# A small FFN on token halves: two column tiles and two row tiles of TensorE, sixteen half-length ReLUs and sums

## What is computed

```python
def ffn(x, Win, bin_, W1, b1, W2, b2, Wout, bout):      # M = 64, INNER = 16
    s = einsum('btd,dm->btm', x, Win) + bin_
    h = relu(s[..., None] * W1 + b1)                     # (tokens, 64, 16)
    g = einsum('btmh,mh->btm', h, W2) + b2
    return einsum('btm,md->btd', g, Wout) + bout

x = x + 0.5 * ffn(layernorm(x), ...)
x = x + attention_and_mlp(layernorm(x), ...)             # DFF = 2048, gelu
x = x + 0.5 * ffn(layernorm(x), ...)
```

## Time and profile before

| | |
|---|---|
| median of 3 runs | 3515.68 us (3514.63 to 3520.36) |
| the profiled execution | 3515.62 us |
| its span, first to last instruction | 3513.6 us |
| mean granted TensorE clock | 0.974 of full |
| TensorE (PE) busy | 3297.1 us, 94% |
| VectorE (DVE) busy | 1833.6 us, 52% |
| ScalarE (ACT) busy | 1322.4 us, 38% |
| GpSimd (POOL) busy | 1154.8 us, 33% |

### The profile page before, as it was taken

The page is one execution under the profiler, slowest core; times in us unless marked ns, Lnnn a source line. Parts: engine busy times, 40 slices in busy tenths (PEclk is TensorE's granted clock), DMA queues, the critical chain, the costliest instruction groups (busy, mean ns, idle before and its releaser), DMA issues. The chain is left out here.

```text
span 3513.6 us, 150217 instructions
## 1 busy us (share of the span) xinstructions
PE 3297.1 (94%) x68430; PEld 2607.9 (74%) x68430; DVE 1833.6 (52%) x2940; ACT 1322.4 (38%) x2630; POOL 1154.8 (33%) x1223
## 2 busy tenths in 40 slices
PE   3999999999959999999978999999999999999997
PEld 2777777777747888888866777777777777777775
DVE  4777777777649777787313332332333233333332
ACT  3544444444313333333333333333333333333332
POOL 0336464646427555555201220212222111122220
PEclk7999999999979999999988999999999999999998
DMA  3344555554466666665552011011100101111010
GB/s 95 109 145 152 155 152 152 152 156 150 131 192 189 194 194 191 195 199 177 171 157 90 13 36 37 24 36 36 37 29 20 36 25 36 37 36 37 13 36 24
DMA packets 388097, 355.41 MB, mean 101 GB/s; under 512 B 58128, under 2 KB 320912, under 8 KB 384912
## 3 DMA queue, kind: packets, MB, share of 16 engines
q1 hardware_dynamic: 385632, 351.27, 32.0%
q10 hardware_dynamic: 2224, 0.90, 0.1%
HBM read 184.19 MB, written 153.09 MB: 96 GB/s over the span
## 5 line engine op out<-in xcount | busy, mean ns | idle before, releaser
L1782 DVE TENSOR_TENSOR glo<-gl,gh 128x512 fp32r<-128x512 f32 x256 | 195.1, 762 | 926.0 <-ACT gh L1689 925.8
L1685 ACT ACTIVATE gl<-bank,b1m 128x512 f32<-128x512 f32 x256 | 175.9, 687 | 796.5 <-PE bank L235 796.5
L233 PE MATMUL bank<-w_hi,gh 128*128 128x512 f32 x1024 | 410.8, 401 | 24.9 <-DVE glo L1782 24.9
L233 PE MATMUL bank<-h_hi,w_hi 128*128 128x512 f32 x1024 | 425.8, 416 | 4.0 <-DVE w_lo L1826 4.0
L235 PE MATMUL bank<-w_hi,glo 128*128 128x512 f32 x1024 | 406.9, 397 | 0.0
L235 PE MATMUL bank<-h_hi,w_lo 128*128 128x512 f32 x1024 | 406.7, 397 | 0.0
L234 PE MATMUL bank<-h_lo,w_hi 128*128 128x512 f32 x1024 | 406.5, 397 | 0.0
L234 PE MATMUL bank<-w_lo,gh 128*128 128x512 f32 x1024 | 405.6, 396 | 0.0
L233 PEld LDWEIGHTS bank<-w_hi,gh 128*128 128x128 f32 x1024 | 193.1, 189 | 75.8 <-DVE glo L1782 31.9
L1187 PE MATMUL bank<-ringA 32*32 32x32 f32 x16512 | 238.7, 196 | 7.7 <-issue 6.1
L233 PEld LDWEIGHTS bank<-h_hi,w_hi 128*128 128x128 f32 x1024 | 193.1, 189 | 58.5 <-issue 10.7
(11 more groups left out here) (170 smaller groups left out, 7071.4 us busy)
## 6 DMA issues: line engine op xcount, KB each, us to landing
ringB<-heads_scratch SPq DMA_DIRECT2D x256, 192.0 KB, 2.7
ringA<-heads_scratch SPq DMA_DIRECT2D x258, 128.0 KB, 2.2
X<-in_L_attn_x SPq DMA_DIRECT2D x16, 1024.0 KB, 9.7
x_scratch<-X SPq DMA_DIRECT2D x16, 1024.0 KB, 4.7
heads_scratch<-vb SPq DMA_DIRECT2D x16, 1024.0 KB, 5.2
heads_scratch<-qk SPq DMA_DIRECT2D x16, 1024.0 KB, 6.9
heads_scratch<-kb SPq DMA_DIRECT2D x16, 1024.0 KB, 5.2
heads_scratch<-kbuf SPq DMA_DIRECT2D x16, 1024.0 KB, 7.1
```

Source lines behind the costliest of these rows:

```text
L233: e.matmul(o, lhs[0], rhs[0], start=first, stop=False)
L1685: e.activation(gl[k][:, :], bank[k][:, :], ACT.Gelu_apprx_tanh, bias=b1m[:, m:m + 1]).then_inc(a_gl, 1)
L1782: e.tensor_tensor(gh[k][1][:, :], gl[k][:, :], gh[k][0][:, :], ALU.subtract).then_inc(v_gl, 1)
```

## The change

- `hidden`: each of the four products becomes two, on columns 0 to 63 of the array for tokens 0 to 255 and on columns 64 to 127 for tokens 256 to 511. The upper and the lower partitions now hold different tokens, and the bank's first 256 columns are used.
- All 16 inner units are now computed on both halves of the partitions: 16 ReLUs and 16 sums of 128 partitions by 256 columns. Four ReLU buffers in place of two; ReLU h waits for sum h - 4.
- `ffn_out`: each of the four products contracts over 64 rows, in the order 0, 2, 1, 3 of the blocks, so that neighbours lie on different row halves and in different banks.
- In the MLP `ffn_out` and `add_ffn` stand at m = 9 and 10 instead of 8 and 9.
- w1t, b1t, w2t have 16 columns; b2t is loaded on both halves (16 loads for 15, without the memset ahead of them).

```diff
+HALF = TOK // 2
+INNER = 16
+FFN_ORDER = (0, 2, 1, 3)
+    def units(pairs):
+        return [2 * q + k for q in pairs for k in range(2)]
...
             def hidden(t):
...
                 for f in range(NF):
-                    m = e.matmul(bank[6][:, :], win[:, f, :], xT3[:, f, :], start=f == 0, stop=f == NF - 1)
+                    for k in range(2):
+                        r = slice(64 * k, 64 * k + 64)
+                        m = e.matmul(bank[6][r, 0:HALF], win[:, f, r], xT3[:, f, k * HALF:(k + 1) * HALF],
+                                     start=f == 0, stop=f == NF - 1)
                 m.then_inc(p_win, 1)
...
+            def ffn_out(t, n):
+                b = FFN_ORDER[n]
+                bk, k = 6 + n % 2, b // 2
+                r = slice(64 * k, 64 * k + 64)
+                if n == 0:
+                    e.wait_ge(v_g3, INNER * t + INNER)
                 bank_free(bk)
-                e.matmul(bank[bk][:, :], g3[:, b * P:(b + 1) * P], wout[:, :],
+                e.matmul(bank[bk][:, :], g3[r, b % 2 * P:(b % 2 + 1) * P], wout[r, :],
                          start=True, stop=True).then_inc(p_wout, 1)
...
-                elif m in (8, 9):
-                    ffn_out(t, 2 * (m - 8))
-                    ffn_out(t, 2 * (m - 8) + 1)
+                elif m in (9, 10):
+                    ffn_out(t, 2 * (m - 9))
+                    ffn_out(t, 2 * (m - 9) + 1)
...
             def relus(t, *hs):
-                for h in hs:
+                for h in units(hs):
...
-                    if 8 * t + h >= 2:
-                        e.wait_ge(v_g3, 8 * t + h - 1)
-                    e.activation(relu3[h % 2][:, :], bank[6][:, :], ACT.Relu, bias=b1t[:, h:h + 1],
+                    if INNER * t + h >= 4:
+                        e.wait_ge(v_g3, INNER * t + h - 3)
+                    e.activation(relu3[:, h % 4, :], bank[6][:, 0:HALF], ACT.Relu, bias=b1t[:, h:h + 1],
                                  scale=w1t[:, h:h + 1]).then_inc(a_relu3, 1)
...
             def sums(t, *hs):
-                for h in hs:
-                    e.wait_ge(a_relu3, 8 * t + h + 1)
+                for h in units(hs):
+                    e.wait_ge(a_relu3, INNER * t + h + 1)
...
-                        e.wait_ge(v_g3, 8 * t + h)
-                        e.scalar_tensor_tensor(g3[:, :], relu3[h % 2][:, :], w2t[:, h:h + 1], g3[:, :],
+                        e.wait_ge(v_g3, INNER * t + h)
+                        e.scalar_tensor_tensor(g3[:, :], relu3[:, h % 4, :], w2t[:, h:h + 1], g3[:, :],
                                                ALU.mult, ALU.add).then_inc(v_g3, 1)
```

More of the change, by code:

```diff
@@ L177, in macaron @@
             hT1 = sbuf(st, "hT_hi", [P, NF, TOK], F32R), sbuf(st, "hT_lo", [P, NF, TOK], F32R)
-            relu1 = [sbuf(st, f"relu{i}", [P, TOK]) for i in range(2)]
-            g1 = sbuf(st, "g1", [P, TOK])
+            relu1 = sbuf(st, "relu", [P, 4, HALF])
+            g1 = sbuf(st, "g1", [P, HALF])
             stats1 = [sbuf(st, f"stats{i}", [P, NB, 6]) for i in range(2)]
@@ L361, in hidden @@
                 for f in range(NF):
-                    m = e.matmul(bank[WIN_BANK][:, :], win[:, f, :], xT1[:, f, :], start=f == 0, stop=f == NF - 1)
+                    for k in range(2):
+                        r = slice(64 * k, 64 * k + 64)
+                        m = e.matmul(bank[WIN_BANK][r, 0:HALF], win[:, f, r], xT1[:, f, k * HALF:(k + 1) * HALF],
+                                     start=f == 0, stop=f == NF - 1)
                 m.then_inc(p_win, 1)
-                released[WIN_BANK] = a_relu, 8 * t + 8
+                released[WIN_BANK] = a_relu, INNER * t + INNER
             def ffn_out(t):
-                e.wait_ge(v_g, 8 * t + 8)
-                for b in range(NB):
-                    bk = 6 + b % 2
+                e.wait_ge(v_g, INNER * t + INNER)
+                for n, b in enumerate(FFN_ORDER):
+                    bk, k = 6 + n % 2, b // 2
+                    r = slice(64 * k, 64 * k + 64)
                     bank_free(bk)
-                    e.matmul(bank[bk][:, :], g1[:, b * P:(b + 1) * P], wout[:, :],
+                    e.matmul(bank[bk][:, :], g1[r, b % 2 * P:(b % 2 + 1) * P], wout[r, :],
                              start=True, stop=True).then_inc(p_wout, 1)
-                    released[bk] = v_x1, 4 * t + b + 1
+                    released[bk] = v_x1, 4 * t + n + 1
             def project(t, j):
@@ L564, in act_project @@
                           (wout[r, :], a["L0_ffn_Wout"]),
[L565 to L568, removed]
+                          (w1t[r, :], W1), (b1t[r, :], B1), (w2t[r, :], W2), (bint[r, :], col(a["L0_ffn_bin_"])),
+                          (b2t[r, :], col(a["L0_ffn_b2"]))]
             for o, s in loads:
@@ L1495, in macaron @@
             ss3 = sbuf(st, "ss3", [P, NB])
-            relu3 = [sbuf(st, f"relu3{i}", [P, TOK]) for i in range(2)]
+            relu3 = sbuf(st, "relu3", [P, 4, HALF])
         stage3 = [xT3[:, f, :] for f in range(NF)] + [Z[1][:, b, :] for b in range(NB)]
@@ L1586, in hidden @@
                 for f in range(NF):
-                    m = e.matmul(bank[6][:, :], win[:, f, :], xT3[:, f, :], start=f == 0, stop=f == NF - 1)
+                    for k in range(2):
+                        r = slice(64 * k, 64 * k + 64)
+                        m = e.matmul(bank[6][r, 0:HALF], win[:, f, r], xT3[:, f, k * HALF:(k + 1) * HALF],
+                                     start=f == 0, stop=f == NF - 1)
                 m.then_inc(p_win, 1)
[L1589 to L1594, removed]
+                released[6] = a_relu3, INNER * t + INNER
+            def ffn_out(t, n):
+                b = FFN_ORDER[n]
+                bk, k = 6 + n % 2, b // 2
+                r = slice(64 * k, 64 * k + 64)
+                if n == 0:
+                    e.wait_ge(v_g3, INNER * t + INNER)
                 bank_free(bk)
-                e.matmul(bank[bk][:, :], g3[:, b * P:(b + 1) * P], wout[:, :],
+                e.matmul(bank[bk][:, :], g3[r, b % 2 * P:(b % 2 + 1) * P], wout[r, :],
                          start=True, stop=True).then_inc(p_wout, 1)
-                released[bk] = v_o, 4 * t + b + 1
+                released[bk] = v_o, 4 * t + n + 1
             def up(t, m):
@@ L1655, in pe_dense @@
                 down(t, NM - 1)
-            for m in range(4, 10):
+            for m in range(4, 11):
                 ffn(NT - 1, m)
@@ L1868, in dve_dense @@
                 add_mlp(t)
-            for m in range(10):
+            for m in range(11):
                 ffn(NT - 1, m)
```

46 lines of the change are left out of this document (23 added, 23 removed).

## The result

| | before | changed |
|---|---|---|
| median | 3515.15 us (3512.27 to 3520.36, 4 runs) | 3554.11 us (3551.46 to 3555.47, 4 runs) |
| profiled execution, its span | 3515.62, 3513.6 us | 3554.45, 3552.5 us |
| mean granted clock | 0.974 | 0.958 |

The ratio is 1.0108, 95% interval 1.0091 to 1.0126. The forecast was 3519 us with a range of 3490 to 3552; the time lies 2 us above the range.

A forecast was written before the change was run, and what follows sets the result against it. TensorE was taken as nearly always busy (99.2 of 100 us in the MLP, 779 of 800 in the projection), its pace set by the small FFN's sums at one place of most tiles. 3515.6 + 17 (projection) - 13 (MLP) = 3519 us, range 3490 to 3552.

The forecast's parts named there:

- a fall of the clock costs 1.0: Projection, ffn_out: after stalls of 3.3 us its products run at clock 0.50, 5.40 us for 4.37.
- t = 1 and 2: +0.2 each: Projection: the second and third token tiles become 0.2 us longer each, part of the projection's 17 us.
- ffn_out gains nothing by itself: Projection: shorter products save nothing at ffn_out, since its third product waits for VectorE's addition to free bank 6.
- The MLP's stall: MLP, before down(7): VectorE and GpSimd take turns of 1.43 us, so TensorE waits 2.5 us for 0.76.
- rival (e): MLP: the stall of 2.5 us lowers the clock each time, 15 x 1.0, giving 3534 us; chance 0.08.
- The array's tilings: TensorE: tiles side by side overlap; hidden takes 2.13 us for 3.45, a pair of last products 1.27 for 1.72.
- (b): Column tiles, which share all rows, don't overlap: +13 and +20 in the projection, 3552 us; chance 0.12.
- (c): Row tiles of the last products don't overlap: +26, giving 3545 us; chance 0.11.
- (d): Products start strictly in program order, holding up the other tile: +13, and +3 in hidden, 3535 us; chance 0.12.
- Rival (a): VectorE and GpSimd share by bytes: MLP stall 0.4 us, -31 there, projection -8, giving 3480 us; chance 0.15.
- The moved unit: MLP: last products one unit later remove the 0.33 us wait; load_z comes later, ScalarE waits up to 1 us, costing nothing.
- The ends: Start and last tile: one more load, sums +2.3, hidden about -2.0, last products about -0.8; together 0.

The follow-up runs named there:

- e4: Changed kernel with GpSimd's additions to Z in each MLP tile held back until the small FFN's last sum is done; 3500.39 us, ratio 0.9961.
- e10: Changed kernel with the projection's ffn_out contracting over all 128 rows, so output differs from the reference; 3532.75 us, ratio 1.0054.
- e5: Kernel before the change, with GpSimd's additions to Z held back until the small FFN's last sum of the tile; 3492.34 us, ratio 0.9933.
- e3: Changed kernel with products nobody reads filling TensorE's waits at ffn_out in the projection and ahead of down(7) in the MLP; 3518.18 us, ratio 1.0008.
- e7: Changed kernel with hidden's products sent as all of one column tile, then all of the other; 3587.62 us, ratio 1.0206.
- e8: Changed kernel with ffn_out's blocks in order 0, 1, 2, 3, so neighbours lie on the same rows; 3592.14 us, ratio 1.0218.
- e12: Projection of before, changed MLP, GpSimd's additions delayed, and the MLP's last products back at m = 8 and 9; 3467.22 us, ratio 0.9862.
- e11: Projection of the kernel before, the change in the MLP, and GpSimd's additions held back until the sums are done; 3464.08 us, ratio 0.9852.
- e1: The change in the MLP alone, projection as in the kernel before, three more small loads; 3519.77 us, ratio 1.0017.
- e2: The change in the projection alone, MLP as in the kernel before, three more small loads; 3552.41 us, ratio 1.0112.

## Why the prediction was wrong

- **The step that failed: "a fall of the clock costs 1.0", in the projection's tiles with a wait of 3.3 us and more, and "t = 1 and 2: +0.2 each".** It had three parts, and each was too small. The fall comes in thirteen of fifteen tiles and not in seven, also where no wait is above 1.3 us; it lasts 6.8 or 10.2 us, through the second pair and nearly all of project(7), and not just while `ffn_out` runs; and each costs about 3 us (e4) for 1.0. In sum it is 21 us by the medians of e10 (25.9 by its profiled execution) beyond the four new falls of 1.0 that the forecast held. The tile from 134.73 to 193.85 us took 59.1, where 56.1 + 0.2 were forecast. The projection's other terms come out nearly right in sum: e10, with all the waits and 128-row products, has seven falls, the number that was forecast, and is 13.4 us later at the end of the projection, where 17 were forecast. Singly they were off: the tiles that should wait 3.9 us for the last sum (t = 4, 7, 10, 13) wait 2.1 to 2.3, and three of e10's seven falls come in other tiles than those named. So the sum is in part luck. The forecast was made from two rows, a wait of 3.3 that lowered the clock and one of 1.2 that did not, both around 128-row products; it took the wait for the cause alone. Not even the wait of 3.3 does it each time: in e5, which has the projection of before, one of three such waits was followed by the lower clock.
- **"ffn_out gains nothing by itself"** was right and not followed to its end: the shorter pair turned into a wait of 1.25 us in the middle (14.0 us in 14 waits). It cost nothing by itself, since the second pair starts 2.4 us after the first either way (154.34 to 156.72, and 154.23 to 156.62 in e10).
- **The MLP's stall: right in each size, wrong in its price.** Turns of 1.43 us, 2.46 us ahead of down(7) for 2.5, no wait before the pairs, 100.4 us a tile: all as worked out, in the four tiles whose clock stays. In the ten others rival (e) came on top, at 1.5 us a tile and not 1.0. In place of -13 the fourteen tiles are +1.6. e3, which leaves VectorE as late and fills the stall, has 100.4 to 100.7 in all of them.
- **The array's tilings: right.** `hidden` was forecast at 2.13 and a pair at 1.27; they show 1.90 and 1.06, but e5's and e4's tiles, neither of which waits, differ by 2.24 us, and 3.43 + 2 x 1.72 - 2.24 = 4.63 is what the three places cost, where 2.13 + 2 x 1.27 = 4.67 was forecast. The changes of tiling beside them are in it. Rivals (b) and (c) are refuted. (d), strict program order, is too for tiles that alternate; e7 and e8 show that order matters all the same, for losing it costs 34 and 38 us, the clock's part in it included.
- **Rival (a), shares by bytes,** is refuted by the turns. By the Trainium skill (SBUF — State Buffer, SBUF: two separate sides) one of the two engines holds the ports for a whole instruction; the turn of 1.43 us agrees, and so does e4, where 7 sums fall from 9.07 to 4.02 us as soon as GpSimd is elsewhere.
- **The moved unit** cost TensorE nothing that the profile shows, as forecast; no run took it back in the changed kernel itself, and e12 against e11, without the stall, shows no difference. ScalarE's squares wait for load_z as worked out, longer than the 1 us named, and TensorE does not notice. From the timeline of ScalarE in the changed kernel, which answers to the earlier trace rows:

```profile
3087.73 0.63 ACT L1684 ACTIVATE H<-Z 128x512 f32<-128x512 f32 x1 [1.72 <-DMA Z<-z_scratch]
```

- **The ends** cost 1, forecast 0; in the last tile the first pair waits 9.95 us for the sums, where the earlier trace rows had 7.46 us, and that is the +2.3 of the sums.

Left open: why 64-row products go with a fall of the clock. e8 against e10 shows that they do, behind a wait for the last sum of 1.3 us and more; without that wait they don't, in the projection (100.45 and 946.11 us in the changed kernel) as in the MLP, whose pairs run at full clock (1.06 us each). No run had products of other row counts than 64 and 128. (The fillers of e3 show that a busier TensorE keeps its clock there.) Nor is it shown what decides in the single tile. The MLP's stall of 2.3 to 2.7 us lowered the clock in eleven of fifteen tiles of the changed kernel and in twelve of e10, whose MLP is the same; in e8 a stall of 2.3 to 2.5 us did so in three of fifteen, and in e7 one of 1.8 to 2.1 us in all. So the length of the stall is not what decides between them.

## What to carry to other kernels

Halving an operation to make TensorE's part cheaper doubles the instructions of the engines that feed it, and where one of these takes turns with another engine, it doubles the turns: here 1.55 us saved at `hidden` (3.45 to 1.90) stand against 1.7 us more of stall (0.76 to 2.46). Price a stall twice, once as idle time and once for the clock behind it, and take the second from rows with the same kind of products; it was here the larger part of the loss. Before giving up such an edit look for what else holds the feeding engine: one wait that sends GpSimd's additions behind the sums turned the MLP's part from +6 us (e1) into -28 (3464.08 of e11 against 3492.34 of e5).

## What the runs showed of the hardware

- The granted clock fell to 0.50 (1.2 GHz) behind two waits of 1.25 and 1.29 us with 64-row products around them (in five of eight such tiles of four runs: the changed kernel, e2, e4, e7), and behind one of 1.25 or 1.30 with the same products one after the other (both tiles of e8); with 128-row products and waits of 1.29 and 1.30 it stayed at 1.00 (both tiles of e10). In the changed kernel's projection it came back after 6.8 or 10.2 us, with TensorE busy since the second pair.
- The Trainium skill (TensorE: Matmul & The Clock Gate, Part 1) states that the clock follows how busy TensorE has been of late. The return behind busy time agrees with it, and so do the fillers of e3.
- In eleven of fifteen MLP tiles of the changed kernel 2.3 to 2.7 us of idle time was followed by the lower clock, in four it was not; in e7 1.8 to 2.1 us was in all fifteen, in e8 2.3 to 2.5 us in three.
- Column tiles that share all rows and row tiles that share all columns overlap all but 0.2 us where they alternate: sixteen instructions of 0.215 us in 1.90 us (1.72 would be full overlap), four of 0.43 in 1.06 (0.86). In blocks, column tiles still overlap in part (2.81 for 3.44 one after the other); neighbours on the same rows don't (a pair takes 1.91, where 4 x 0.43 is 1.72).
- Halving the columns brings a ReLU of the projection from 774 to 567 ns (the earlier trace rows and below) and a sum there from 875 to 540 on the mean, from the changed kernel's groups by line (busy time, mean ns of one, idle before):

```profile
L519 ACT ACTIVATE relu<-bank,b1t,w1t 128x256 f32<-128x256 f32 x256 | 126.8, 567 | 26.7 <-PE bank L373 21.8 <-DVE g L701 3.9
L701 DVE SCALAR_TENSOR_TENSOR g<-relu,w2t,g 128x256 f32<-128x256 f32 x240 | 129.7, 540 | 21.1 <-ACT relu L519 1.0
```
